# Moving the first expert choice, the early ordering and two evictions in the attention groups of a fused language-model layer

## The reference

```python
h = tok_embed(x)                                   # embedding row (179) + projection of a 64-point STFT (77)
h = h + local_attention(layernorm(h), Wq, bq, ...) # each token sees itself and 2 neighbours on each side
h = h + moe(layernorm(h), router_w, ...)           # 8 experts, top 2, capacity 1280 assignments each

# moe, for T = 4096 tokens of 256 numbers
probs = softmax(xf @ router_w + router_b)
topk_p, topk_i = top_k(probs, 2); topk_p /= topk_p.sum(-1)
rank = place of the assignment among those of its expert; keep = rank < cap
h = gelu(einsum('ecd,edf->ecf', buf, w1) + b1)     # 256 -> 512
eo = einsum('ecf,efd->ecd', h, w2) + b2            # 512 -> 256
out[token] += eo * weight
```

## Time and profile before

| | us |
|---|---|
| median of 3 runs | 380.99 |
| lowest, highest | 379.92, 382.88 |
| the profiled execution, time | 382.53 |
| the profiled execution, span | 380.7 |
| PE busy | 326.0 (86%) |
| DVE busy | 259.0 (68%) |
| ACT busy | 209.2 (55%) |
| POOL busy | 205.0 (54%) |

### The profile page before, as it was taken

The page is one execution under the profiler, slowest core; times in us unless marked ns, Lnnn a source line. Parts: engine busy times, 40 slices in busy tenths (PEclk is TensorE's granted clock), DMA queues, the critical chain, the costliest instruction groups (busy, mean ns, idle before and its releaser), DMA issues.

```text
span 380.7 us, 9114 instructions
## 1 busy us (share of the span) xinstructions
PE 326.0 (86%) x2616; PEld 269.0 (71%) x2616; DVE 259.0 (68%) x836; ACT 209.2 (55%) x481; POOL 205.0 (54%) x156
## 2 busy tenths in 40 slices
PE   0689998987978969596999779999999999999970
PEld 0646767665756647374888558888888888888860
DVE  4955456579887986898676457667667677676650
ACT  1634794687869764662455335555555555555530
POOL 5015460000575775777787644584856555655761
PEclk9999996899889975989899999999999999999996
DMA  6999778795273444948499877686978668644552
GB/s 136 322 306 382 240 271 359 300 401 199 84 266 129 157 151 126 220 145 201 132 131 179 139 115 101 103 105 94 130 102 116 86 102 122 102 43 56 58 57 28
DMA packets 82268, 61.85 MB, mean 162 GB/s; under 512 B 55843, under 2 KB 75844, under 8 KB 80780
## 3 DMA queue, kind: packets, MB, share of 16 engines
q1 hardware_dynamic: 68462, 42.64, 42.1%
q0 software_dynamic: 13760, 18.63, 28.2%
HBM read 15.75 MB, written 35.27 MB: 134 GB/s over the span
## 4 chain that ended last, share of the span: by engine, by line
PE 57%; DVE 15%; DMA 14%; issue 4%; ACT 3%; SPq 3%; POOL 2%; POOLq 0%; ACTq 0%; DVEq 0%
PE bank L1691 22%; PE bank L1678 21%; DMA inv_rows<-reg_a 6%; DMA reg_a<-inv_rows 4%; DMA out<-reg_h,meta 3%; PE bank L1572 3%; PE bank L1574 2%; POOL out L593 2%; SPq L471 1%; PE bank L1387 1%; PE bank L1558 1%; DVE reg_a L852 1%; DVE reg_h L1323 1%; PE bank L1398 1%; DVE reg_z L1250 1%
## 5 line engine op out<-in xcount | busy, mean ns | idle before, releaser
L593 POOL DMA_INDIRECT out<-reg_h,meta x74 | 115.9, 1566 | 68.2 <-DMA out<-reg_h,meta 31.9
L1678 PE MATMUL bank<-reg_z,w1s 128*128 128x256 f16 (+1 forms) x936 | 111.9, 269 | 4.6 <-ACT reg_a L792 3.8
L1691 PE MATMUL bank<-w2s,reg_h 128*128 x888 | 111.0, 276 | 2.8 <-DVE reg_h L1323 2.8
L572 POOL DMA_INDIRECT slot_rows<-reg_z,slots x64 | 66.5, 1039 | 68.2 <-DVE reg_z L1250 51.2
L1678 PEld LDWEIGHTS bank<-reg_z,w1s 128*128 x936 | 88.7, 99 | 16.8 <-issue 5.8
L1691 PEld LDWEIGHTS bank<-w2s,reg_h 128*128 128x128 f16 x888 | 87.1, 99 | 14.8 <-issue 3.9
L792 ACT ACTIVATE reg_a<-bank,b1s 128x256 f32<-128x256 f32 (+1 forms) x156 | 70.3, 463 | 30.9 <-PE bank L1678 27.4
L804 ACT ACTIVATE reg_h<-bank,meta 128x256 f32<-128x256 f32 x74 | 35.1, 474 | 72.5 <-PE bank L1691 65.0
L1329 DVE SCALAR_TENSOR_TENSOR reg_h<-reg_w,meta,reg_h 128x256 f32<-128x256 f32 x74 | 35.9, 485 | 48.4 <-ACT reg_h L804 46.0
L1323 DVE SCALAR_TENSOR_TENSOR reg_h<-reg_a,reg_h 128x256 f16<-128x256 f32 (+1 forms) x156 | 64.7, 415 | 5.4
L1321 DVE TENSOR_SCALAR reg_h<-reg_a 128x256 f16<-128x256 f32 (+1 forms) x156 | 46.7, 299 | 9.7 <-ACT reg_a L792 7.0
(11 more groups left out here) (231 smaller groups left out, 359.7 us busy)
## 6 DMA issues: line engine op xcount, KB each, us to landing
slot_rows<-reg_z SPq DMA_DIRECT2D x8, 1360.0 KB, 9.2
reg_h<-w SPq DMA_DIRECT2D x12, 512.0 KB, 9.3
out<-reg_p SPq DMA_DIRECT2D x8, 512.0 KB, 3.3
reg_w<-w SPq DMA_DIRECT2D x4, 512.0 KB, 10.8
out<-reg_z SPq DMA_DIRECT2D x1, 1280.0 KB, 15.4
out<-reg_h,meta POOLq DMA_INDIRECT x74
reg_a<-inv_rows SPq DMA_DIRECT2D x6, 193.5 KB
reg_a<-masks SPq DMA_DIRECT2D x1, 1056.0 KB, 11.2
```

Source lines behind the costliest of these rows:

```text
L572: nc.gpsimd.indirect_dma_start(out=slot_rows, out_offset=bass.IndirectOffsetOnAxis(ap=slots[:, side, n:n + 1], axis=0), in_=x2w[:, n % RIN ...
L593: nc.gpsimd.indirect_dma_start(out=out.rearrange("t p c -> (t p) c"), out_offset=bass.IndirectOffsetOnAxis(ap=meta[:, p, s, 0:1], axis=0), ...
L1678: last = mm(bank[(0, 2, 3)[n % 3]][:, 0:rows_of(p)], w1s[:, wp, bass.ds(expert[p], 1), kt, j * P:(j + 1) * P].rearrange("p e c -> p (e c)" ...
L1691: last = mm(bank[4 + n % 4][:, 0:H], hT[:, p % 2, hp, f, s * P:(s + 1) * P], w2s[:, wp, bass.ds(expert[p], 1), f, :].rearrange("p e c -> p ...
```

## The change

Five edits:

1. ACT, routing groups: tiles 0 and 1 are evicted ahead of the first `exps`; the last two `exps` come behind all evictions. Other groups keep the alternation.
2. DVE: `first_choice(c)` leaves the end of groups 1, 3 and 5 and stands in groups 2, 4 and 6 behind `scores(g + 1)`.
3. DVE: `order_early` is split. Its first instruction, the one that reads the totals, stays at the end of group 5 (`read_totals`); the rest stands in group 6 behind `first_choice`.
4. PE and ACT, prologue: `scores(1)` leaves the start of group 0 and stands between `turn_probs(0)` and `turn_values`. ACT's `copy_g(1)`, whose result it reads, moves from behind `copy_prT(0)` to behind `copy_ut(0)`.
5. PE, expert stage: the last chunk's `rank` and `count_late` come behind `layer1(1, 1)` instead of `layer1(1, 0)`.

```diff
@@ ACT attend(g)
-                    for t in range(TPG):
-                        exps(g + 1, t)
-                        evict(g, t)
+                    if ended(g - 1):
+                        evict(g, 0)
+                        evict(g, 1)
+                        exps(g + 1, 0)
+                        evict(g, 2)
+                        exps(g + 1, 1)
+                        evict(g, 3)
+                        exps(g + 1, 2)
+                        exps(g + 1, 3)
+                    else:
+                        for t in range(TPG):
+                            exps(g + 1, t)
+                            evict(g, t)
@@ ACT prologue
             copy_ut(0)
+            copy_g(1)
             pair_high(11)
             copy_prT(0)
-            copy_g(1)
@@ DVE
-            def order_early():
+            def read_totals():
                 have = totals.unsqueeze(2).to_broadcast([NU, E, UPE])
                 dve.wait_ge(totals_done, 1)
                 tt(under.rearrange("u (e j) -> u e j", j=UPE), have, of_units(C_FULL), ALU.is_ge).then_inc(totals_read, 1)
+
+            def order_early():
+
                 dve.wait_ge(totals_read, 1)
@@ DVE attend(g)
                     scores(g + 1)
+                for c in ended(g - 1):
+                    first_choice(c)
                 if more2:
                     normed(g + 2)
+                if g == 6:
+                    order_early()
...
                 if g == 5:
-                    order_early()
+                    read_totals()
                 for c in ended(g):
                     deviation(c)
-                    first_choice(c)
@@ PE attend(g)
-                if more:
+                if g and more:
                     scores(g + 1)
@@ PE prologue
             turn_probs(0)
+            scores(1)
             turn_values()
@@ PE expert stage
-                    if (p, j) == (1, 0):
+                    if (p, j) == (1, 1):
                         rank(len(CHUNKS) - 1)
                         count_late()
```

## The result

| | before | after |
|---|---|---|
| median of 20 runs each, us | 380.38 | 383.84 |
| lowest, highest | 376.68, 387.13 | 380.31, 388.93 |
| mean | 380.43 | 384.16 |
| profiled execution, span | 380.7 | 382.1 |
| mean granted clock in it | 0.942 | 0.930 |

The change makes the kernel slower, by 0.95%, just inside the 1% that a measurement of it can tell. The forecast was 380.5 us with 383.5 as its upper end; the median lies 0.3 us above that end. It is the side of rival C (383.0), and, as will be seen, not quite by its mechanism. Medians and means take every execution; the ratio and its 95% interval leave out those more than 1.5% above the fastest of their kernel.

A forecast was written before the change was run, and what follows sets the result against it. The end was taken to hang on when group 6 gives POOL chunk 2. Terms -2.0 + 0.3 + 1.0 + 0.25 = -0.45 us, set on the median 380.99, gave 380.5 us, range 377.6 to 383.5.

The forecast's parts named there:

- rival C: Chance 0.15: leading evictions hold the exponentials, 1.4 us in group 4, 0.55 for two small waits, prologue 0: 383.0 us.
- What bounds the kernel: The end moves with when group 6 gives chunk 2 to POOL; PE time saved behind group 6 doesn't count.
- Waits are moved, not removed: Groups 2 and 6: PE's eviction waits of 1.08 and 3.16 us return as longer waits before turn_probs.
- rival B: Chance 0.10: removed PE waits of 1.08 + 3.16 us count in full, plus prologue's 3.4, less 1.0: 374.4 us.
- +0.3 and +0.25: Groups 2 and 6: DVE, reordered, waits briefly for PE's scores, making the kernel 0.3 and 0.25 us later.
- +1.0, group 4: Two exps behind the last eviction end later, delaying DVE's probs and ACT: 1.0 us slower, bounds 0 and +1.4.
- -2.0, the prologue: Group 0: scores(1) moved into a PE wait brings turn_probs(1) earlier; 2.0 us gain taken between 0 and 3.4.
- 0 for the clock: No term in the sum; gathered waits lowering the clock cost about 0.5 us in group 2, only within rival C.
- 0 for edit 5: Expert stage: one more layer1 step, some 0.7 us, fits PE's 3.79 us wait for counts, so no cost or gain.

## Why the prediction was wrong, step by step

**What bounds the kernel.** That the end moves with the time at which POOL gets chunk 2 was right. Over the 12 profiles of the faster chips, the span rises by 0.96 us for each us by which that first scatter is later (correlation 0.77), and by 0.95 for each us of POOL's fifteenth output scatter (0.95). What the frame left out is the stretch from the first to the fifteenth output scatter, which takes 33.3 to 36.3 us, a spread as large as most effects here.

**Waits are moved, not removed (rival B out).** Right. The profile shows 3.07 and 4.23 us at L1563, and DVE runs to the probabilities without a pause behind its scores.

**+0.3 and +0.25, DVE waits for the scores.** Right in kind, too small: 0.42 and 0.50 us. Group 4 has the same wait, 0.54, and the sum had none there. 1.46 in place of 0.55: 0.9 us missed. No run isolated these waits, so what they cost in the whole is argued from the trace.

**+1.0, group 4.** The mechanism exists (edit 1 alone, 2.62 us at L989). In the changed kernel's profile it costs nothing, the lower bound that the prediction named, but not because `first_choice` covers it: the other two profiles with all five edits have waits of 3.33 and 3.36 us. The prediction took the last tile's time, 116.25, as given "whatever the order". It hung on PE's hold of 2.33 us, and this on the load of `b2`. What the term costs on average is open; in an execution the slow group 3 and this wait exclude each other, as far as the profiles show.

**-2.0, the prologue: the step that failed most.** One execution was read as the kernel. The clock had fallen in the profile's group 0 and doesn't in every execution to the same extent; the prediction wrote that case down (the edit then gives 0) and took a value near the middle of the profiled execution's gain all the same. In the one profile of the changed kernel the group did give 2.51 us; over the profiles it is 1.0 +- 0.6, and in the time of the kernel edit 4 alone measured -0.1 +- 0.6 us.

**0 for the clock: the step that failed most after it.** The rule of gathered waits stood in rival C at 0.5 us and in the sum at nothing. Measured, the change has some 9 us more at the half clock (53.5 against 43.0 to 45.3 of the kernel before in three sets). What is a us of it worth? Filling the waits, which changes the clock and, apart from spare work that runs over, nothing that is due, gave 1.6 us for 15.3, 1.9 for 9.1 and 3.7 for 19.3 on the faster chips: 0.11, 0.21 and 0.19. So 9 us are worth about 1.5, an estimate with an error of about 0.5. It is a mean over stretches that cost much and stretches that cost nothing: half clock in groups 3 and 5 makes them longer, half clock behind POOL's first output scatter was not seen to. Among executions of the kernel before the slope is 0.33 +- 0.03 (92 executions), but there a stall makes both a longer time and a slower clock, so it isn't the price.

The Trainium skill, "TensorE: Matmul & The Clock Gate", section "HAM oscillation — how this bites in real kernels", warns that idle gaps in a loop let the clock fall each time round. The trace of the changed kernel agrees: 3.07 and 2.41 us of waiting, then 0.73 and 0.74 over groups 3 and 5. It doesn't happen each time: with edit 1 alone on the same kind of chip, waits of 2.69 and 1.85 us were followed by 0.92 and 1.00. The prediction quoted the rule, and priced only the products right behind the wait instead of the whole next group, and that as a rival.

**0 for edit 5.** Not borne out, and not refuted: 1.0044 and 1.0036 alone. PE's wait ahead of the rank was 3.05 us (3.79 before), so the cover was there. Why it should cost is open.

**The sum again.** With the measured terms, DVE's three waits (1.46), the clock (about 1.5), edit 4 (-0.1) and edit 5 (0 to 1.4) make 2.9 to 4.3 us, against +3.7 +- 0.8. The agreement is partly luck: the 1.46 us are read off one trace, and group 4's term is left out. By parts it adds up as well. Averaging both chips with their weights, edit 1 measured +1.9 +- 0.8, edits 2 and 3 +1.3 +- 0.8, edit 4 -0.1 +- 0.6 and edit 5 +1.2 +- 0.6, together +4.2 +- 1.4. Each part for itself is near the limit of what was told apart; that edit 1 alone costs, and through what, is not shown. A version that beats the kernel before isn't shown either: the four kernels with parts of the change and fillers differ from it by -2.0 to -0.8 us in the means, each by less than twice its error.

## What to carry to other kernels

Before a wait is moved behind another, ask what PE does in the group that *follows*: a gathered wait can leave its own group shorter and the next one, where PE is the bound, 2 to 4 us longer at the half clock. Then ask what the group after that waits for: here a load that came at its own time gave back what group 3 had lost in one execution, and brought a new wait where group 3 was fast. Don't take a gain from a slow-clock stretch of one profiled execution; look whether the stretch is in others too, since here half the profiles without the edit had it in full and the others a shorter one or none. If PE must wait anyway, spare matmuls inside the wait are a cheap test of whether the clock is the cause, and they should end before the awaited data comes.

## What was not expected of the hardware

With ten spare matmuls (2.32 us) in group 2's wait, group 3 was granted 1.00 in all three such profiles of the faster chips, though 0.92 us of idling stayed; in the four without them, behind 3.07 or 3.08 us of idling, it was granted 0.66 to 0.88. And half clock is not loss: most of what the changed kernel's profile had more of it lies where nothing was seen to be later for it. Executions of one and the same kernel range over 10 us (376.68 to 387.13 in 20 runs). The faster ones spend less time at the half clock (correlation 0.73 in 92 executions of the kernel before), so much of this range goes together with the clock, whichever causes the other.
